# A gated mixture kernel: the last half expert's rows reach their tokens by matmuls with ones and zeros, and three engines share the final combination in halves

## The reference

```python
x = L0_attn_x                       # [8, 512, 256]
xn = _layernorm(x, axis=-1)
s = _L0_attn_ref(xn, ...)           # chunked gated linear attention, 16 heads, RMS norm, @ Wo
g = _silu(_L0_ffn_ref(xn, ...))     # mixture of 8 experts
x = x + s * g
```

```python
affinity = softmax(einsum('bsd,ed->bse', x, gate_w)).transpose(0, 2, 1)
gating, idx = top_k(affinity, 128)
x_in = x[bidx, idx]
h = silu(x_in @ w_gate[e].T) * (x_in @ w_up[e].T)      # 1024 hidden features
x_e = h @ w_down[e].T
out = zeros_like(x).at[bidx, idx].add(gating[..., None] * x_e)
```

## Time and profile before

| | |
|---|---|
| Time, median of 3 runs | 858.71 us (857.99 to 860.87) |
| Profiled execution: time, span | 857.91 us, 856.0 us |
| TensorE (PE) busy | 788.5 us, 92% |
| VectorE (DVE), ScalarE (ACT), GpSimd (POOL) busy | 549.4, 502.4, 412.6 us |
| Mean granted clock of TensorE | 0.96 |
| Last read of s issued | 807.84 us |
| Scatter of the first half of the last expert ends on GpSimd | 801.3 us |
| Last instruction of VectorE ends | 849.95 us |

### The profile page before, as it was taken

The page is one execution under the profiler, slowest core; times in us unless marked ns, Lnnn a source line. Parts: engine busy times, 40 slices in busy tenths (PEclk is TensorE's granted clock), DMA queues, the critical chain, the costliest instruction groups (busy, mean ns, idle before and its releaser), DMA issues.

```text
span 856.0 us, 17481 instructions
## 1 busy us (share of the span) xinstructions
PE 788.5 (92%) x6484; PEld 681.0 (80%) x6484; DVE 549.4 (64%) x1031; ACT 502.4 (59%) x1150; POOL 412.6 (48%) x361
## 2 busy tenths in 40 slices
PE   7716999999999999999999999999999999999950
PEld 5514788888888888888888888888888888888840
DVE  6786566666656766666666676666567666556567
ACT  5676665666566655666566655665466555654431
POOL 7564643556254715563265625472455435470221
PEclk9767899999999999999999999999999999999985
DMA  8368997777566766686577757676566667562939
GB/s 273 115 219 257 257 372 204 151 185 200 166 137 192 153 208 158 172 201 194 151 150 193 179 178 159 164 181 208 157 165 196 179 168 219 174 133 93 281 92 284
DMA packets 137605, 160.85 MB, mean 188 GB/s; under 512 B 11824, under 2 KB 108592, under 8 KB 137520
## 3 DMA queue, kind: packets, MB, share of 16 engines
q1 hardware_dynamic: 124800, 142.91, 55.6%
q0 software_dynamic: 12288, 16.79, 12.1%
q10 hardware_dynamic: 432, 0.04, 0.0%
HBM read 117.48 MB, written 42.21 MB: 187 GB/s over the span
## 4 chain that ended last, share of the span: by engine, by line
PE 85%; DVE 6%; SPq 1%; ACT 1%; POOL 1%; issue 1%; DMA 1%; DVEq 0%; POOLq 0%; ACTq 0%
PE y_ps L1523 21%; PE g_ps L1495 20%; PE up_ps L1495 20%; PE m_ps L1387 5%; PE a_ps L1447 4%; PE o_ps L1483 3%; PE m_ps L1431 3%; PE m_ps L1405 2%; PE m_ps L1424 2%; PE o_ps L1472 1%; PE m_ps L1415 1%; DVE e_row L1270 1%; PE m_ps L1397 1%; DMA lb_row<-lb_tiles 1%; PE o_ps L1455 1%
## 5 line engine op out<-in xcount | busy, mean ns | idle before, releaser
L1495 PE MATMUL up_ps<-xgt,w_r 128*128 128x512 f32 x768 | 206.3, 404 | 0.0
L1523 PE MATMUL y_ps<-w_r,hid_r 128*128 128x256 f32 x1536 | 204.8, 283 | 0.7 <-DVE hid_r L1351 0.7
L1495 PE MATMUL g_ps<-xgt,w_r 128*128 128x512 f32 x768 | 200.2, 396 | 0.5 <-DVE sg L1335 0.5
L1335 DVE SCALAR_TENSOR_TENSOR sg<-sg,g_ps 128x512 f32<-128x512 f32 x128 | 87.7, 685 | 168.7 <-ACT sg L1106 161.8
L1523 PEld LDWEIGHTS y_ps<-w_r,hid_r 128*128 128x128 f32 x1536 | 192.7, 190 | 1.7 <-DVE hid_r L1351 0.9
L811 POOL TENSOR_TENSOR w_r<-w_raw,w_r 128x768 fp32r<-128x768 f32 x64 | 123.7, 1934 | 104.1 <-ACT w_r L1016 103.8
L1495 PEld LDWEIGHTS up_ps<-xgt,w_r 128*128 128x128 f32 x768 | 139.2, 189 | 28.1
L1495 PEld LDWEIGHTS g_ps<-xgt,w_r 128*128 128x128 f32 x768 | 136.6, 190 | 23.3 <-DVE sg L1335 0.7
L1106 ACT ACTIVATE sg<-g_ps 128x512 f32<-128x512 f32 x128 | 76.4, 597 | 121.0 <-PE g_ps L1495 111.8
L837 POOL DMA_INDIRECT ffn_dram<-y_sb,idx_all x64 | 105.1, 1642 | 75.1 <-DVE y_sb L1257 59.3
L806 POOL TENSOR_SCALAR_AFFINE_SELECT lb_row<-lb_row 128x1024 f32<-128x1024 f32 x64 | 78.1, 1229 | 85.2 <-DMA lb_row<-lb_tiles 85.1
(11 more groups left out here) (246 smaller groups left out, 1009.3 us busy)
## 6 DMA issues: line engine op xcount, KB each, us to landing
lb_row<-lb_tiles SPq DMA_DIRECT2D x64, 512.0 KB
w_raw<-w_experts SPq DMA_DIRECT2D x64, 384.0 KB
qk_dram<-qk_r SPq DMA_DIRECT2D x32, 512.0 KB, 4.5
k_st<-qk_dram SPq DMA_DIRECT2D x96, 128.0 KB
arena<-qk_dram SPq DMA_DIRECT2D x192, 64.0 KB
x_all<-x SPq DMA_DIRECT2D x8, 512.0 KB, 9.6
xn_dram<-x_all SPq DMA_DIRECT2D x8, 512.0 KB, 5.9
e_row<-lb_tiles SPq DMA_DIRECT2D x64, 64.0 KB
```

The source lines that it names most:

```text
L1335: dve.scalar_tensor_tensor(out=sg[:, :], in0=sg[:, :], scalar=1.0, in1=g_ps[:, :], op0=ALU.add, op1=ALU.mult).then_inc(t_done, 1)
L1495: mm = pe.matmul(bank[:, :], w_r[:, m, a, at:at + P], xgt[:, b, k, half * 512:(half + 1) * 512], start=(j == 0 and k == 0), stop=(j == len ...
L1523: mm = pe.matmul(y_ps[:, j, :], hid_r[p][:, a, j * P:(j + 1) * P], w_r[:, m, b, DOWN:DOWN + D], start=(m == 0 and q == 0 and j % 2 == 0), ...
```

## The change

- `slot_at` holds, for the last expert and batches 4 to 7, the number within its sequence of each chosen token. GpSimd writes the numbers 0 to 511 (`numbers`) and compares them with slot_at, one comparison per batch, into `ones_at`: 128 chosen rows by 512 tokens, one where the row belongs to the token.
- The scatter of the last half expert and the reads behind it are gone. Instead VectorE and ScalarE gate two tiles of y_ps each (`last_sums`, `y_high`), and TensorE multiplies ones_at with y_sb (`to_tokens`), two matmuls per half batch, so that `f_ps` holds what the last half expert adds to each token. VectorE adds this to what ffn_dram held before (`whole`).
- All eight batches of ffn_dram are read during the last steps of the loop, each as two transfers; batches 4 to 7 land in `f_late`, space of the experts' inputs and weights that is free by then.
- ScalarE multiplies s by r1 in place, in SBUF, eight ACTIVATEs in each of the iterations u = TS + 4 to TS + 7, behind the copy of hid (`scale_s`). `combine` had this factor in its product.
- The final combination is done in halves of 128x512. ScalarE takes SiLU of a half (`result`); VectorE does the product and the sum of batches 0, 5, 6, 7 and the product of batch 4, GpSimd the sum of batch 4 and both of batches 1, 2, 3, in the order 1, 2, 4, 3. The stores keep the order 0 to 7, each after both halves.
- `g_of` takes turns over five buffers; batches 5 and 6 use again those of 1 and 2, and batch 7 uses y_sb.

The diff, without declarations of semaphores and passing of arguments:

```diff
@@ -90,6 +90,8 @@
+        with ExitStack() as lent:
+            plain = sb_in(lent)("plain", [P, NT * D])
@@ -499,7 +501,7 @@
-        return f32(arena[:, first:first + words])
+        return plain[:, first:first + words]
@@ -538,9 +540,14 @@
+        slot_at = sb("slot_at", [P, TPB])
...
-        f_at = [f32(w_r[:, b, :, :]).rearrange("p l n -> p (l n)")[:, 0:TPB * D] for b in range(B)]
+        w_left = f32(w_r[:, :, :, :]).rearrange("p m l n -> p m (l n)")
+        f_late = [f32(xgt[:, l, :, 0:512]) for l in range(2)] + [w_left[:, 2 * n:2 * n + 2, TPB * D:] for n in range(2)]
+        f_at = [w_left[:, b, 0:TPB * D].rearrange("p (h n) -> p h n", h=2) for b in range(TPB)] + f_late
@@ -559,9 +566,17 @@
-        g_row = [e_row[:, :, :].rearrange("p k n -> p (k n)"), small[:, :]]
-        g_of = [g_row[0], g_row[1]] * 2 + [g_row[0], g_row[1], y_sb[:, :, :].rearrange("p t d -> p (t d)"), g_row[0]]
+        def in_halves(ap):
+            return [ap[:, h * 512:(h + 1) * 512] for h in range(2)]
+        g_row = [in_halves(t) for t in (e_row[:, :, :].rearrange("p k n -> p (k n)"), small[:, :],
+                                        y_sb[:, :, :].rearrange("p t d -> p (t d)"))] \
+            + [[w_raw[h][:, 0:512] for h in range(2)],
+               [t[:, :, :].rearrange("p t h -> p (t h)") for t in (neg_lb, exp_rest)]]
+        g_of = [g_row[n] for n in (0, 1, 3, 4, 0, 1, 3, 2)]
+        numbers = w_raw[0][:, 0:N]
+        ones_at = [dec_more[:, 0, :], dec_more[:, 1, :], dec_last[:, :, :].rearrange("p h n -> p (h n)"), th[:, :]]
@@ -570,6 +585,8 @@
+        f_ps = [a_ps[:, :, :].rearrange("p h n -> p (h n)"), o_ps[:, :], m_ps[:, :], g_ps[:, :], up_ps[0][:, :], up_ps[1][:, :],
+                y_ps[:, 0:2, :].rearrange("p t d -> p (t d)"), y_ps[:, 2:4, :].rearrange("p t d -> p (t d)")]
@@ -706,11 +729,13 @@
                 def fetch_f(b):
-                    sp.dma_start(f_at[b].rearrange("p (t d) -> p t d", t=TPB),
-                                 ffn_dram[b * N:(b + 1) * N, :].rearrange("(t p) d -> p t d", p=P)).then_inc(f_in[b], 16)
+                    for h in range(2):
+                        at = b * N + h * N // 2
+                        sp.dma_start(f_at[b][:, h, :].rearrange("p (t d) -> p t d", t=2),
+                                     ffn_dram[at:at + N // 2, :].rearrange("(t p) d -> p t d", p=P)).then_inc(f_in[b], 16)
                 def store_out(b):
-                    sp.wait_ge(o_done, b + 1)
+                    sp.wait_ge(finished[b], 2)
@@ -785,16 +810,18 @@
                         fetch_s(B - 1)
+                        sp.wait_ge(up_done, XS - MI)
+                        sp.wait_ge(scattered, 16 * TPB * (2 * E - 2))
+                        for n in range(F_EARLY, F_EARLY + 2):
+                            fetch_f(n)
...
                         fetch_f(u - TS - 3)
+                    if u in (TS + 5, TS + 6):
+                        fetch_f(F_EARLY + u - TS - 3)
...
                         load_lb((u + 4) // 2)
-                sp.wait_ge(dn_done, XS)
-                for n in range(F_EARLY, B):
-                    sp.wait_ge(last_out[n - F_EARLY], 16)
-                    fetch_f(n)
@@ -838,7 +865,7 @@
                             in_=y_sb[:, t, :], in_offset=None, compute_op=ALU.add)\
-                            .then_inc(last_out[t] if n == 2 * E - 1 else scattered, 16)
+                            .then_inc(scattered, 16)
@@ -918,15 +945,38 @@
                         scatter(n // MI - 1)
+                    if u == TS + 2:
+                        pool.wait_ge(av_done, NT)
+                        pool.iota(numbers, pattern=[[1, N]], base=0, channel_multiplier=0,
+                                  allow_small_or_imprecise_dtypes=True).then_inc(numbered, 1)
+                        pool.wait_ge(numbered, 1)
+                        pool.wait_ge(slots_set, 1)
+                        for t in range(TPB):
+                            pool.tensor_scalar(ones_at[t], numbers, slot_at[:, t:t + 1], None, ALU.is_equal).then_inc(ones_set, 1)
...
                         low(block_of(u))
-                scatter(2 * E - 1)
-                for t in range(TPB):
-                    pool.wait_ge(last_out[t], 16)
+                pool.wait_ge(x_in, 16 * B)
+                pool.wait_ge(s_scaled, B * TPB)
+                def finish(f, h):
+                    n = 2 * (f - 1) + h
+                    pool.wait_ge(g2_done, 2 * f + h + 1)
+                    pool.tensor_tensor(g_of[f][h], g_of[f][h], half(s_at[f], h), ALU.mult).then_inc(scaled_pool, 1)
+                    pool.wait_ge(scaled_pool, n + 1)
+                    pool.tensor_tensor(half(x_at[f], h), g_of[f][h], half(x_at[f], h), ALU.add).then_inc(finished[f], 1)
+                for f in (1, 2):
+                    for h in range(2):
+                        finish(f, h)
+                for h in range(2):
+                    pool.wait_ge(scaled_dve, 2 + h + 1)
+                    pool.tensor_tensor(half(x_at[TPB], h), g_of[TPB][h], half(x_at[TPB], h), ALU.add).then_inc(finished[TPB], 1)
+                for h in range(2):
+                    finish(3, h)
@@ -1060,6 +1110,17 @@
+                def scale_s(f):
+                    if f == 0:
+                        act.wait_ge(s_in, 16 * B)
+                        act.wait_ge(r_step, 7)
+                    if f >= B:
+                        return
+                    for t in range(TPB):
+                        at, tile = slice(t * D, (t + 1) * D), f * TPB + t
+                        act.activation(s_at[f][:, at], s_at[f][:, at], ACT.Identity, scale=r1[:, tile:tile + 1]).then_inc(s_scaled, 1)
@@ -1142,14 +1203,29 @@
                         act.activation(r0[:, :], ln_ms[:, :], ACT.Exp, scale=-0.5).then_inc(r_step, 1)
-                for f in range(B):
-                    act.wait_ge(f_in[f], 16)
-                    if f == F_EARLY + 2:
-                        for t in range(TPB):
-                            act.wait_ge(last_out[t], 16)
-                    elif f >= 2:
-                        act.wait_ge(o_done, f - 1 if f < F_EARLY + 2 else F_EARLY + 1)
-                    act.activation(g_of[f], f_at[f], ACT.Silu).then_inc(g2_done, 1)
+                    if u > TS + 3:
+                        scale_s(2 * (u - TS - 4))
+                        scale_s(2 * (u - TS - 4) + 1)
+                def result(f, h):
+                    if f < TPB:
+                        act.wait_ge(f_in[f], 32)
+                        if f == 2:
+                            act.wait_ge(ones_set, TPB)
+                        act.activation(g_of[f][h], f_at[f][:, h, :], ACT.Silu).then_inc(g2_done, 1)
+                    else:
+                        act.wait_ge(f_whole, 2 * (f - TPB) + h + 1)
+                        act.activation(g_of[f][h], g_of[f][h], ACT.Silu).then_inc(g2_done, 1)
+                for h in range(2):
+                    result(0, h)
+                act.wait_ge(dn_done, XS)
+                for t in range(2, TPB):
+                    act.activation(y_sb[:, t, :], y_ps[:, t, :], ACT.Identity,
+                                   scale=gate_all[:, E - 1, TPB + t:TPB + t + 1]).then_inc(y_high, 1)
+                for f in range(1, B):
+                    for h in range(2):
+                        result(f, h)
@@ -1203,6 +1279,7 @@
+                        dve.tensor_tensor(slot_at[:, :], at_a[:, TPB:, E - 1], apart[:, TPB:, E - 1], ALU.add).then_inc(slots_set, 1)
@@ -1258,20 +1335,45 @@
-                def combine(f):
-                    if f == 0:
-                        dve.wait_ge(x_in, 16 * B)
-                        dve.wait_ge(s_in, 16 * B)
-                    dve.wait_ge(g2_done, f + 1)
-                    g = g_of[f]
-                    for t in range(TPB):
-                        at = slice(t * D, (t + 1) * D)
-                        tile = f * TPB + t
-                        ins = dve.scalar_tensor_tensor(out=g[:, at], in0=g[:, at], scalar=r1[:, tile:tile + 1],
-                                                       in1=s_at[f][:, at], op0=ALU.mult, op1=ALU.mult)
-                    ins.then_inc(c_step, 1)
-                    dve.wait_ge(c_step, f + 1)
-                    dve.tensor_tensor(x_at[f], g, x_at[f], ALU.add).then_inc(o_done, 1)
+                def scale(f, h):
+                    dve.wait_ge(g2_done, 2 * f + h + 1)
+                    dve.tensor_tensor(g_of[f][h], g_of[f][h], half(s_at[f], h), ALU.mult).then_inc(scaled_dve, 1)
+                def finish(f, h):
+                    dve.wait_ge(scaled_dve, (0 if f == 0 else 2 * (f - TPB + 1)) + h + 1)
+                    dve.tensor_tensor(half(x_at[f], h), g_of[f][h], half(x_at[f], h), ALU.add).then_inc(finished[f], 1)
+                def whole(f, h):
+                    n = 2 * (f - TPB) + h
+                    dve.wait_ge(f_in[f], 32)
+                    if f == 4:
+                        dve.wait_ge(finished[0], 2)
+                    elif f in (5, 6):
```

(46 more changed lines are left out.)

13 lines of the change are left out of this document (9 added, 4 removed).

## The result

The changed kernel takes 868.84 us (median of 4 runs, 868.01 to 870.28) against 858.9 for the kernel before beside it: a ratio of 1.0117, 95% interval 1.0098 to 1.0135. It is slower by 9.9 us; the forecast was 871.0. The profiled execution has a span of 866.3 (time 868.01).

A forecast was written before the change was run, and what follows sets the result against it. TensorE was taken to bound the kernel up to the last matmul, then VectorE's arithmetic the tail. T 831.7 plus a tail of 37.3 gave span 869.0, forecast 871.0 us against a median of 858.7 before; range 863 to 880.

The forecast's parts named there:

- The sum: Whole kernel: span 831.7 + 37.3 = 869.0, execution 1.9 more, median 0.8 above that; stated as 871.0 us, 1.4% slower.
- The scalings: Last four loop steps: eight ScalarE ACTIVATEs take 3.33 us, a step 6.08 instead of 4.22, delaying TensorE by 6.2.
- T: Moment the experts' last down projection is finished: 825.5 before, predicted 831.7 after the change.
- Rival C: Slower last loop steps: TensorE's clock falls to 1.2 GHz, one to three steps 2.3 us longer each, 873 to 878; chance 0.15.
- The comparisons beside r1: GpSimd's iota and four comparisons are hidden; VectorE's four small steps for r1 beside them lose 0.2 us in all.
- Rival D: Small steps for r1: each waits for a GpSimd comparison, 3.2 us later in all, 874; chance 0.12.
- lies in the wait for s: Before the first scaling: the 0.2 us delay of r1's small steps is hidden, as ScalarE waits for s until 811.0.
- Where the tail starts: After the last down projection: last scalings end T + 0.8, first SiLU follows the table load at T + 2.1, GpSimd starts T + 5.5.
- Turns of VectorE and GpSimd: Tail: VectorE's 18 instructions with both inputs in SBUF and GpSimd's 14 do not overlap; VectorE ends at T + 32.4.
- Rival B: Tail: GpSimd and VectorE share freely, with ScalarE as in the main forecast; span 865.8, time 868; chance 0.15.
- The last store: End of the tail: the last store lands some 4.8 us after its issue, at T + 37.3.
- The removed scatter and late reads at 0: Tail: the removed GpSimd scatters and late reads of ffn_dram were hidden beside VectorE's batches, so removing them gains 0.

The follow-up runs named there:

- e3: Changed kernel, but in batches 4 to 7 VectorE's products and sums take their second input from PSUM, leaving s and x out: 866.77 us.
- e4: Changed kernel with buffers of their own for batches 5 and 6, so VectorE doesn't wait for GpSimd's batches 1 and 2: 873.01 us.
- e5: Changed kernel with sum, SiLU and product of batches 4 to 7 in their PSUM bank, batch 4's sums on VectorE: 864.34 us.
- e7: Kernel before (scatter and late reads stay) with ScalarE's scalings of s alone, VectorE's product one instruction of 128x1024 per batch: 866.88 us.
- e8: e7 with the scalings split, four behind the tanh and four behind the copy of hid: 861.45 us.
- e6: e5 with scalings four and four in both ScalarE gaps, stores ordered 0, 1, 4, 5, 2, 6, 3, 7, comparisons behind r1's last small step: 855.99 us.
- e9: e6 with the scalings of batches 6 and 7 moved behind SiLUs that ScalarE does in the tail: 854.11 us.
- e11: e9 with the first scaling waiting for seven reads of s, the eighth waited for ahead of batch 7: 851.29 us, ratio 0.9903.

## Why the prediction was right, step by step

- **The sum.** By its own terms it gives 871.7 (870.9 + 0.8), not 871.0; the forecast was 2.2 too high, and 2.9 by its terms.
- **The scalings.** Eight at 3.33, measured 3.31. A step at 6.08, measured 5.83: a scaling and the tanh each start 0.1 before the end of what stands ahead of them. The tanh of 127 was put at 826.5 and came at 826.47. This agreement is partly luck: M was 0.4 later, r1's steps 0.7 later, and the scalings themselves shifted the last down projection by only 5.0 (6.14 in all). The waits in front of the gate matmuls of 126 and 127 were put at 1.5 to 2 each and measured 0.36 and 1.31: the first 1.3 of the tanh's delay went into the gap of 1.3 that the prediction itself names, and behind a wait TensorE's three groups took 4.52 (816.17 to 820.69), not 4.22.
- **T.** 831.7 against 832.9. The 1.2 is the low clock in the last down projection. Rival C named the mechanism, but put it in whole steps of 2.3 each; it struck one group of twelve matmuls. It delays nothing on ScalarE, whose last scalings end at 832.38 with the table load behind them: from S to GpSimd's first product it is 24.64 to 24.65 in the changed kernel, e3, e4 and e5, while the last down projection took 2.93, 2.93, 1.75 and 2.06. So it only moves 1.2 from the tail to the loop.
- **The comparisons beside r1.** 0.2 predicted, hidden; 0.75 measured, and it reached the gate matmuls. Rival D's 3.2 was far off: the first two of the four steps weren't held at all, and the last ended 0.8 before the comparison that it ran beside. The step that failed in this profile is "lies in the wait for s": r1 was ready at 806.31, but its delay had reached the copy of hid ahead of the scalings, which ended just as the read landed, so there was no wait for s to hide it. In e3, e4 and e5, with the same loop, there was one (0.58, 0.57, 1.48), and there the step held.
- **Where the tail starts.** First SiLU at T + 2.1, measured T + 0.8; GpSimd at T + 5.5, measured T + 3.4. The last scalings were put to end at T + 0.8 and ended at T - 0.5, since T itself was late; that is 1.3 of the 2.1. The rest: ScalarE's instructions overlap by 0.1 each, and GpSimd's first product ran beside batch 0's sums (1.82) and didn't wait for them.
- **Turns of VectorE and GpSimd.** Predicted from two pairs of rows, shown by e3 and e5. Batch 1 took 5.7 (5.4 predicted), batch 2 5.9 (6.2), GpSimd's last six 9.6 (9.8), VectorE's rest to the last store 5.2 (5.6). Rival B, free sharing, has the nearest time (868) and the wrong mechanism.
- **The last store.** 4.8 predicted from its issue to the end, 3.7 measured; its transfer is listed with 3.2. Together with the earlier start this makes the tail 33.4 instead of 37.3, the term of the sum that was most in error, by 3.9; T was off in the other direction by 1.2, and the two errors share that 1.2.
- **The removed scatter and late reads at 0.** Right for this sum. But e7 shows them as a second bound at the same place: with VectorE's end 1.5 earlier the tail stayed as it was. So the matmuls with ones and zeros are worth something only in company: e8, which has the cheap scalings and keeps the scatter, stays at 861.45, while e6 with the matmuls (and with GpSimd's share, the sums in PSUM and the other order of the stores) is at 855.99. No run takes the matmuls alone.

What remains open: why the clock fell in e6 and e8 (waits of 1.89 and 1.88 ahead of the last down projection, and before that 0.74 and 0.57 in front of a group of gate matmuls) and not in e9 (1.89, and none before). No run varied it by itself. It is also open why the time ahead of M differs by up to 4 us between executions. And e6, e9 and e11 join several edits; the order of the stores was never run alone.

## What to carry to other kernels

Work moved to an engine with idle time has to fit into its gaps one by one: ScalarE was busy 60% of the span, but eight scalings in a row (3.3 us) between a copy and the next tanh cost 6.2 in the loop, while two groups of four cost 0.5 there; the last eight, left together, still cost 2.4 in the tail. When VectorE and GpSimd take turns over operands in SBUF, as here, give VectorE one operand in PSUM (e3, e5) before giving it fewer instructions; taking away a wait between them can make it worse (e4, by 2.0). And when a gain doesn't show, look at which second chain ends at the same place: the comparisons behind r1 paid nothing until the wait for the eighth read was moved.
